# A gated cross-attention and quantised feed-forward block on one core: second layer norm from row sums and ScalarE squares, and the opening's queues in another order

## What is computed

```python
q1 = fake_quant(layernorm(x), s1, z1)        # 8 bit, whole numbers 0..255
q2 = fake_quant(ctx, s2, z2)
x = x + tanh(g_xattn) * (q1 @ q2)            # per batch of 512 rows
v = layernorm(x)                             # mean and variance over 1024 columns
A, g = quant_act(v)       # one scale g = max|v| / 2688; fp8 per block of 16; last 128 columns twice
gate, up = A @ int4(Wg).T * g, A @ int4(Wu).T * g    # int4 per block of 16
h = silu(gate) * up
Am, gm = quant_act(h)
out = x + tanh(g_ffn) * (Am @ int4(Wd).T * gm)
```

## Time and profile before

| | us |
|---|---|
| median of 3 runs | 871.32 (870.17 to 871.70) |
| the profiled execution's own time | 870.89 |
| its span | 869.0 |
| TensorE busy | 738.5 (85%) |
| VectorE busy | 617.9 (71%) |
| GpSimd busy | 356.6 (41%) |
| ScalarE busy | 305.8 (35%) |

### The profile page before, as it was taken

The page is one execution under the profiler, slowest core; times in us unless marked ns, Lnnn a source line. Parts: engine busy times, 40 slices in busy tenths (PEclk is TensorE's granted clock), DMA queues, the critical chain, the costliest instruction groups (busy, mean ns, idle before and its releaser), DMA issues.

```text
span 869.0 us, 10408 instructions
## 1 busy us (share of the span) xinstructions
PE 738.5 (85%) x3478; PEld 336.5 (39%) x3483; DVE 617.9 (71%) x1006; ACT 305.8 (35%) x370; POOL 356.6 (41%) x194
## 2 busy tenths in 40 slices
PE   1488300399999999999999999999698799999998
PEld 0234100154544444444444444444243344444443
DVE  5789999999265656565757676732699999989710
ACT  3657595333133434344434343520122122211100
POOL 4992789523156666666657585820000000000000
PEclk9998755599999999999999999999799999999999
DMA  8810757733449796979797979843224665663420
GB/s 315 312 50 34 209 173 190 170 64 80 75 95 210 162 220 159 222 163 232 162 220 168 228 165 220 185 104 116 98 42 118 164 158 151 174 151 101 101 58 24
DMA packets 228355, 131.36 MB, mean 151 GB/s; under 512 B 201312, under 2 KB 212576, under 8 KB 227296
## 3 DMA queue, kind: packets, MB, share of 16 engines
q1 hardware_dynamic: 228320, 130.92, 61.8%
HBM read 61.88 MB, written 19.66 MB: 94 GB/s over the span
## 4 chain that ended last, share of the span: by engine, by line
PE 73%; DVE 19%; POOL 4%; DMA 2%; issue 1%; ACT 1%; SPq 0%; DVEq 0%; ACTq 0%
PE acc L1218 48%; PE acc L1273 24%; POOL big L688 2%; DVE big L1484 2%; DVE tb L1393 1%; DVE big L1488 1%; PE acc L1154 1%; DVE big L1366 1%; DVE bst L1315 1%; DVE big L1468 1%; DVE tb L1473 1%; DMA mid<-wbuf 1%; DVE h_in L1417 1%; POOL mid L690 1%; DMA big<-in_x_dram 1%
## 5 line engine op out<-in xcount | busy, mean ns | idle before, releaser
L1218 PE MATMUL acc<-mid 128*128 128x512 f16 x1920 | 415.2, 379 | 0.8 <-DVE h_out L1505 0.8
L1218 PEld LDWEIGHTS acc<-mid 128*128 128x128 f16 x1920 | 187.7, 98 | 227.2 <-DVE h_out L1505 1.2
L1273 PE MATMUL acc<-big,mid 128*128 128x512 f16 x1056 | 232.1, 383 | 9.7 <-DMA mid<-wbuf 8.6
L779 POOL TENSOR_TENSOR h_in<-wbuf,h_in 128x1024 f16<-128x1024 f32 (+1 forms) x56 | 114.4, 2044 | 113.1 <-ACT h_in L1056 113.0
L1273 PEld LDWEIGHTS acc<-big,mid 128*128 128x128 f16 x1056 | 103.7, 99 | 137.5 <-issue 9.1
L696 POOL TENSOR_TENSOR wbuf<-wbuf,w_inv 128x1024 f32<-128x1024 f32 (+1 forms) x67 | 124.9, 1870 | 39.9 <-DVE w_inv L1399 39.9
L1505 DVE SCALAR_TENSOR_TENSOR h_out<-acc,gs,silu 128x256 f32<-128x256 f32 (+1 forms) x88 | 41.7, 474 | 121.7 <-ACT silu L908 95.7
L1393 DVE TENSOR_REDUCE tb<-wbuf 128x64 f32<-128x1024 f32 (+1 forms) x67 | 79.0, 1179 | 40.3 <-DMA wbuf<-in_L_ffn_w_gate_dram 21.5
L1056 ACT ACTIVATE h_in<-wbuf 128x1024 f16<-128x1024 f32 (+1 forms) x56 | 57.0, 1019 | 119.1 <-DVE wbuf L1405 119.1
L858 ACT ACTIVATE wbuf<-wbuf 128x1024 f32<-128x1024 f32 (+1 forms) x67 | 68.1, 1016 | 82.8 <-POOL wbuf L696 82.0
L1218 PE MATMUL acc<-big,mid 128*128 128x384 f16 x192 | 33.4, 336 | 48.1 <-DMA mid<-big 48.1
(11 more groups left out here) (161 smaller groups left out, 616.4 us busy)
## 6 DMA issues: line engine op xcount, KB each, us to landing
h_in<-h_d SPq DMA_DIRECT2D x8, 1376.0 KB, 7.0
wbuf<-in_L_ffn_w_gate_dram SPq DMA_DIRECT2D x21, 512.0 KB, 4.2
wbuf<-in_L_ffn_w_up_dram SPq DMA_DIRECT2D x21, 512.0 KB, 4.1
h_d<-h_out SPq DMA_DIRECT2D x80, 128.0 KB, 3.4
big<-in_ctx_dram SPq DMA_DIRECT2D x16, 512.0 KB, 7.0
wbuf<-in_L_ffn_w_down_dram SPq DMA_DIRECT2D x16, 512.0 KB, 4.5
big<-in_x_dram SPq DMA_DIRECT2D x8, 512.0 KB, 6.7
x_d<-big SPq DMA_DIRECT2D x8, 512.0 KB, 3.0
```

Of the source, the lines that this page charges most:

```text
L779: pool.tensor_tensor(nat[s % 4][:, H:H + cols], wbuf[:, s % 4, 0:cols], nat[s % 4][:, 0:cols], ALU.subtract)\
L1218: last = pe.matmul(acc[m % 4][:, 0:cols], left[:, k, s * P:(s + 1) * P], w[:, right, k, 0:cols], start=(k == 0 and left is a_hi and right ...
L1273: last = pe.matmul(acc[2 * i + hf][:], amT[:, i, k // DH, left, k % DH, :], right[:, k, hf * MW:(hf + 1) * MW], start=(k == 0 and left == ...
```

## The change

- The second layer norm no longer uses `bn_stats`. `make_x1` lets its two VectorE instructions also give their row sums (`accum_out`), one small VectorE instruction makes the negative mean of the tile, and ScalarE squares the tile with that mean as bias and gives the sum of squares (`square_x1`, written over `hm`, which is not yet in use). `spread_x1` makes the variance from it, where `aggregate` stood.
- `layernorm` takes five small VectorE instructions in place of seven for the second layer norm, and six in place of eight for the first.
- `start_a` has one VectorE instruction over 1024 columns where two over 512 stood.
- Pieces 7 to 11 are handled later: their `front` stood between `start_a(0)` and `end_a(2)` and now stands behind `end_a(6)`, the last of them behind P4. The `front` of piece 6 stood ahead of g and now stands behind `start_a(0)`. The matching steps of ScalarE, GpSimd and SP move with them.
- All eight x tiles are loaded ahead of the first ctx tile, and the order of nearly every queue in the first two stages is new. On GpSimd the clip of an even ctx tile is no longer followed at once by its shift. TensorE does `row_sums` ahead of `attend(4)`. VectorE does `clip_ctx(15)` and `quantise_x(4)` around `make_x1(0)`, `max_a(0..3)` and `a_coef_unbound` earlier.

```diff
+            def square_x1(t):
+                act.wait_ge(mean_ready, t + 1)
+                if t >= 1:
+                    act.wait_ge(x1_squared, t)
+                act.activation(square_out, x_all[:, t, :], ACT.Square, bias=n_mean[:, t:t + 1], accum_out=x_sq[:, t:t + 1])\
+                    .then_inc(x1_squared, 1)
...
+            def spread_x1(n, ts):
+                dve.wait_ge(x1_squared, ts.stop)
+                dve.tensor_scalar(ve[:, ts], x_sq[:, ts], 1.0 / H, EPS, ALU.mult, ALU.add).then_inc(var_ready, 1)
...
                 dve.wait_ge(sqrt_done, n)
-                step(dve.reciprocal(r, sq[:, ts]))
-                step(dve.tensor_tensor(r, r, ve[:, ts], ALU.mult))
-                step(dve.tensor_tensor(r, r, sq[:, ts], ALU.add))
-                step(dve.tensor_scalar(r, r, 0.5, None, ALU.mult))
-                step(dve.reciprocal(m, r))
-                if mul is not None:
-                    step(dve.tensor_scalar(m, m, mul, None, ALU.mult))
-                step(dve.tensor_tensor(r, m, mv[:, ts, 0], ALU.mult))
-                dve.tensor_scalar(ln_add[:, ts], r, -1.0, 0.0 if add is None else add, ALU.mult, ALU.add).then_inc(ln_ready, 1)
+                step(dve.tensor_tensor(r, sq[:, ts], sq[:, ts], ALU.mult))
+                step(dve.tensor_tensor(r, r, ve[:, ts], ALU.add))
+                step(dve.reciprocal(r, r))
+                step(dve.scalar_tensor_tensor(out=m, in0=r, scalar=mul, in1=sq[:, ts], op0=ALU.mult, op1=ALU.mult))
+                if add is None:
+                    dve.tensor_tensor(ln_add[:, ts], m, n_mean[:, ts], ALU.mult).then_inc(ln_ready, 1)
+                else:
+                    step(dve.tensor_tensor(r, m, mv[:, ts, 0], ALU.mult))
+                    dve.tensor_scalar(ln_add[:, ts], r, -1.0, add, ALU.mult, ALU.add).then_inc(ln_ready, 1)
...
                     last = dve.scalar_tensor_tensor(out=xs, in0=acc[pair(t) + hf][:], scalar=tt[:, 0:1], in1=xs,
-                                                    op0=ALU.mult, op1=ALU.add)
+                                                    op0=ALU.mult, op1=ALU.add, accum_out=x_sum[:, t, hf:hf + 1])
                 last.then_inc(x1_ready, 1)
                 dve.wait_ge(x1_ready, t + 1)
-                return stats(t)
+                dve.tensor_scalar(n_mean[:, t:t + 1], x_sum[:, t, 0:1], x_sum[:, t, 1:2], -1.0 / H, ALU.add, ALU.mult)\
+                    .then_inc(mean_ready, 1)
...
                 dve.wait_ge(ro_ready, t + 1)
-                for hf in range(2):
-                    v, nb = xn_all[:, t, hf * MW:(hf + 1) * MW], MW // BLK
-                    last = dve.scalar_tensor_tensor(out=blocks(v), in0=spread(a_coef[:, t % 4, hf * nb:(hf + 1) * nb]),
-                                                    scalar=gs[:, 6:7], in1=blocks(v), op0=ALU.min, op1=ALU.mult)
-                step(last)
+                v = blocks(xn_all[:, t, :])
+                step(dve.scalar_tensor_tensor(out=v, in0=spread(a_coef[:, t % 4, :]), scalar=gs[:, 6:7], in1=v,
+                                              op0=ALU.min, op1=ALU.mult))
```

More of the change, by code:

```diff
@@ L771, in _ @@
             lo_a(5)
+            scale(7, 0)
+            scale(8, 1)
+            back_open(7)
+            back_open(8)
+            lo_open(7)
+            lo_open(8)
             lo_a(6)
+            scale(9, 2)
             lo_a(7)
+            scale(10, 3)
+            back_open(9)
+            scale(11, 0)
+            lo_open(9)
+            back_open(10)
+            lo_open(10)
             def lo_nat(u, s):
@@ L1023, in _ @@
             silu_open(("P", 1))
[L1024 removed]
+            floor_a(4)
             silu_open(("U", 0))
             silu_open(("U", 1))
+            floor_a(5)
+            silu_open(("P", 2))
+            silu_open(("P", 3))
             floor_a(6)
[L1028 removed]
+            silu_open(("U", 2))
             hi_a(4)
             hi_a(5)
[L1031 removed]
+            round_w(7, 0)
             floor_a(7)
[L1033 removed]
+            whole_w(7)
+            round_w(8, 1)
+            whole_w(8)
+            hi_open(7)
             silu_open(("U", 3))
+            hi_open(8)
+            hi_a(6)
             silu_open(("P", 4))
[L1036 removed]
+            hi_a(7)
             silu_open(("P", 5))
[L1038 removed]
+            round_w(9, 2)
+            whole_w(9)
             silu_open(("U", 4))
+            round_w(10, 3)
+            whole_w(10)
+            hi_open(9)
             silu_open(("U", 5))
+            round_w(11, 0)
             silu_open(("P", 6))
+            hi_open(10)
             silu_open(("P", 7))
@@ L1195, in _ @@
             attend(2)
+            turn_x(4)
+            attend(3)
             col_sums(1, 3)
-            attend(3)
-            turn_x(4)
+            turn_x(5)
             col_sums(1, 4)
-            turn_x(5)
+            turn_x(6)
             col_sums(1, 5)
+            turn_x(7)
             col_sums(1, 6)
             col_sums(1, 7)
-            turn_x(6)
-            turn_x(7)
+            row_sums()
             attend(4)
-            row_sums()
             attend(5)
@@ L1546, in _ @@
             step(first_stats(3))
+            first_stats(6)
+            aggregate(slice(0, 4))
+            dve.wait_ge(idx_loaded, 32)
+            dve.wait_ge(consts_made, 1)
+            nm = I // 64
+            dve.tensor_tensor(neq[:, 0:8], idx[:, 0:8], iot[:, 0:8], ALU.not_equal).then_inc(flag_step, 1)
+            dve.tensor_tensor(neq[0:64, 8:8 + nm], idx[0:64, 8:8 + nm], iot[0:64, 8:8 + nm], ALU.not_equal).then_inc(flag_step, 1)
+            dve.wait_ge(flag_step, 2)
+            dve.tensor_reduce(nfl[:, 0:1], neq[:, 0:8], AX_X, ALU.max).then_inc(flag_step, 1)
+            dve.tensor_reduce(nfl[0:64, 1:2], neq[0:64, 8:8 + nm], AX_X, ALU.max).then_inc(flag_step, 1)
+            layernorm(1, slice(0, 4), tt[:, 5:6], prm[:, 1:2])
+            clip_ctx(1)
+            first_stats(4)
+            quantise_x(0)
+            clip_ctx(3)
+            quantise_x(1)
             dve.wait_ge(flag_step, 5)
@@ L1601, in _ @@
             front_open(5)
-            step(max_a(5))
-            a_coef_unbound(slice(0, 4), step)
+            max_a(5)
             step(max_a(6))
-            front_open(6)
             dve.tensor_reduce(gpart[:, 0:1], bmx[:, 0:NT - 1, :].rearrange("p t b -> p (t b)"), AX_X, ALU.max)
@@ L1653, in _ @@
             step(end_a(6))
-            h_open(("U", 1))
+            front_open(7)
             start_a(7)
-            h_open(("P", 2))
+            front_open(8)
+            step(end_a(7))
             h_open(("P", 3))
-            step(end_a(7))
+            fold_outliers(6)
             h_open(("U", 2))
-            fold_outliers(6)
+            front_open(9)
             h_open(("U", 3))
+            front_open(10)
             h_open(("P", 4))
+            front(PIECE_LOOP, 0, 16 * (loads_before(0, 0) + 1), looped=True)
             h_open(("P", 5))
```

318 lines of the change are left out of this document (146 added, 172 removed).

## The result

| | before | after |
|---|---|---|
| median, us | 870.75 (869.1 to 871.7, 4 runs) | 864.73 (864.45 to 865.15, 4 runs) |
| profiled span, us | 869.0 | 862.7 |
| ratio after / before | | 0.9928, 95% interval 0.9909 to 0.9947 |

The change makes the kernel 0.7% faster, 6.0 us. The forecast was 864.3, with a range of 858.0 to 870.5.

What follows compares the result with a forecast made beforehand. VectorE was taken to bound the opening and TensorE the rest. The stage terms ended the opening at 235.2, 7.0 us earlier: 870.9 - 7.0 = 863.9 profiled, 0.4 below the median, so 864.3 us, range 858 to 870.5.

Steps and rivals of the forecast that it cites:

- What bounds the kernel: Whole kernel: VectorE bounds the opening, TensorE the rest; only the start of the loop's first product, 242.2 us, counts.
- First stage: Loads to col_lo(1): first clip at 18.9, first make_x1 near 57.5, VectorE enters the second stage 3.9 us late at 79.9.
- Second stage: From col_lo(1) to start_a(0): 38.0 us instead of 45.4, so start_a(0) at 117.9 instead of 121.4.
- rival e: ScalarE's squares beside the roots: Square needs table loads, about 2.5 us on the path, 866.8 us; chance 0.03.
- Front 6: VectorE's second stage: front(6) leaves the stretch ahead of g, -2.0 us for its instructions.
- Third stage: From start_a(0) to the taking out of U2 on VectorE: 88.1 us, U2 out at 206.0 to 206.5.
- TensorE: Opening products: P0 at 150 instead of 166.9, waits of 4, 3 and 2 us, U4 at 206.5.
- From U4 to the end: Opening's last six products: U4, U5, P6, P7, U6, U7 take 28.7 us, ending at 235.2, 7.0 earlier.
- The late pieces: Piece 10 from front to landed transpose: 21 us, landing at 232.7, 2.5 ahead of TensorE's need.
- rival b: Loop start: late pieces decide; a 30.1 us path gains only 0.4, 34 us gives 875; chance 0.17 of at least 3 us.
- Rival (c): Second stage: first stage's 5 us not earned back before g, start_a(0) at 121.4, end at 867.8; chance 0.14.
- Rival (d): Opening products: TensorE, not held by VectorE, runs through from P0 at 150, giving 854; chance 0.05.

Runs made afterwards that it cites:

- b_arith: The kernel before with every queue order kept and only the change's arithmetic added; 872.34 us, ratio to before 1.0014.
- b_sums: The kernel after with the queue orders of before from front 6 on, and x and ctx loads interleaved again; 876.35 us, ratio to before 1.0057.
- a_oldorder: The kernel after with the queue orders of the kernel before from front 6 on, word for word; 879.92 us, ratio to before 1.0101.
- b_late: The kernel before with only pieces 7 to 11 moved to their late places on all four queues; 868.28 us, ratio to before 0.9962.
- a_bnstats: The kernel after with bn_stats and aggregate back for the second norm and no squares, shorter inverse root kept; 876.52 us, ratio to before 1.0056.
- a_clip: The kernel after with interleaved x and ctx loads and the clip of ctx tile 8 moved from GpSimd to VectorE; 856.19 us, ratio to before 0.9837.
- a_extra2: The kernel after with two idle reductions added on VectorE behind the taking out of P4; 864.54 us, ratio to before 0.9922.
- a_ctx: The kernel after with ctx tiles again loaded between x tiles and the first statistics ordered to match; 860.70 us, ratio to before 0.9876.
- a_extra1: The kernel after with two idle reductions added on VectorE behind end_a(7), ahead of P3's take-out; 865.99 us, ratio to before 0.9937.
- a_split: The kernel after with start_a's scaling again as two instructions of half a tile; 865.50 us, ratio to before 0.9927.
- a_early: The kernel after with pieces 7 to 11 handled early again, one slot later than in the kernel before; 874.56 us, ratio to before 1.0042.
- a_takeout: The kernel after with P3, U2 and U3 taken out early, fold(6) left in place, other queues following; 868.28 us, ratio to before 0.9959.

## Why the prediction was right

The table of U6 has a simple reading. From P0 to U6 the kernels in which TensorE runs on without a pause take 64.3 to 65.1 us (before 64.8, b_arith 64.5, b_sums 65.1, a_oldorder 64.3). From `start_a(0)` to U6 those with late pieces take 108.5 to 110.8 (b_late 108.5, after 109.1, a_bnstats 109.1, a_clip 109.3, a_extra2 109.3, a_ctx 110.3, a_extra1 110.7, a_split 110.8). So there are two limits to the opening's end, and the later one counts: P0 plus 65, and `start_a(0)` plus 109 (the spread of 2.3 us has the slower clock of a_split and a_ctx in it, and the added work of a_extra1). Before, the first gives 231.7 and the second would give 229.9 or so: GpSimd, with all pieces ahead of `lo_a(0)`, was the limit, and VectorE lay 1.8 us behind it. a_early fits neither (72.3 and 118.5) and has waits in both parts; a_takeout is the one with the late tile 6.

Point by point, by the steps of the prediction:

- **What bounds the kernel.** "The opening belongs to VectorE" is the step that was half wrong. From 121.3 to 166.9 GpSimd is busy 42.65 of 45.60 us, about as full as VectorE, and it ends what TensorE waits for: `hi_a(0)` is done at 153.0, and `lo_a(0)` starts at 160.12, 7.1 us later, behind the pieces. The row stood there, and I read its VectorE column. The sum came out right because the change moves both limits at once. By the sentence as it stands the arithmetic alone would have gained several us; b_arith gained none. There the gain was already gone at `start_a(0)`, in waits for attention and the squares; in b_sums `start_a(0)` was 2.9 us earlier than before, and P0 still 4.6 later.
- **First stage.** The first clip was forecast at 18.9 and came at 19.20. The first `make_x1` came at 59.50 and not at 57.5: VectorE waited 7.31 us for `col_out(0)` and had the second norm, two clips and `quantise_x(4)` behind it, which I had as done already. `col_lo(1)` was done at 78.6 against 79.9. So VectorE enters the second stage 1.3 us earlier than forecast. The load order was said to make this stage 3.9 us late; a_ctx puts its price at 4.9 at `start_a(0)`.
- **Second stage.** Forecast 38.0 us up to `start_a(0)`; it took 37.3, from 78.60 to 115.88. Accumulators cost nothing on VectorE (0.08 us each, in the shadow of the next instruction), a mean step 0.13 before the next one starts. ScalarE's squares take 1.15 and 0.19 for the read-out, and no table load stands beside one (rival e). The trace agrees with the rule cited from the Trainium skill (SBUF — State Buffer, Who interferes with whom) as far as small steps go that stretch with GpSimd beside them: in `layernorm(4)` one step took 1.57 us and its quiet like 0.16, and it ended at 102.85, as GpSimd's instruction did at 102.84. Three such rows appear in a_bnstats; the shorter root has fewer steps that can be caught.
- **Front 6.** Counted at -2.0 for its instructions. In a_oldorder and b_sums it also waited 7.4 and 7.1 us for its load, because that load is issued 6 to 11 us later under the new order and the stage reaches it 4 to 9 us sooner. Moving it behind `start_a(0)` avoids that: the load is issued at 113.46 in the kernel after, and front 6 runs at 118.39 without a wait. It is worth more than the term that the sum had for it, and the kernel before could not show it.
- **Third stage.** Forecast 88.1 us to the taking out of U2, measured 89.9 (115.88 to 205.75): `start_a` saves 1.0 and not 1.6, and `end_a`'s last instruction takes 14.2 us over the eight tiles against 12.9. That U2 comes at 205.75 against 206.0 is luck in part: `start_a(0)` was 2.0 us early, and this stage 1.8 longer.
- **TensorE.** P0 at 148.72 against 150, waits of 3.43, 2.94 and 2.41 us against 4, 3 and 2, U4 at 206.28 against 206.5, last `silu` at 235.57 against 235.2.
- **From U4 to the end.** The step "what follows is U4, U5, P6, P7, U6, U7" held by 0.34 us. Tile 7 landed just then, which the sum had not looked at, so this was a near thing; a_takeout shows that with U4 11 us earlier the end isn't earlier at all. The chain goes through `fold(6)` and SP.
- **The late pieces.** Path of piece 10: 22.0 us against 21, landed at 233.4 against 232.7. It did not bind there (rival b), nor in a_clip, where TensorE runs on without a gap from U6 at 216.57.

Rival (c), `start_a(0)` past 121, did not come in the kernel after. Its cause is real in the old order: in b_arith VectorE waits 4.7 us for squares, and `start_a(0)` is at 121.79. a_bnstats and a_oldorder get past 121 by other causes, at 126.5 and 123.9. Rival (d), TensorE running through from P0, is what the kernel before did and what b_arith and b_sums still do, from a late P0.

What stays open: how much of the 15 us between a_oldorder and after goes to front 6's wait and how much to GpSimd's queue, since the two were not undone one by one in that pair. The shorter root and the new order of the first two stages were not tried each by itself. That SP's transpose of piece 8 ahead of `turn_a(7)` costs up to 2 us is read from the chain and was not tried.

## What to carry to other kernels

Work taken off an engine can turn into waits on the same engine if the queues are laid out for the old durations: all the new arithmetic was worth 0 in the old order, its statistics alone were worth 11 us in the new one, and with the new order only ahead of front 6 it was 9 us slower than no change. So time the arithmetic and the order together, and again one by one to find the part that costs (here the load order, 4.5 us).

Before naming the engine that bounds a stage, read all the busy columns of its window and add up, from each, the way to the stage's end; here two engines, busy 93% and 97% of a stretch, were two limits, 1.8 us apart. An earlier start of one group was worth nothing here while an input of the last groups came as late as before.
